# Local attention in a 13-stage decoder: queries and keys made with tokens on partitions, normalised and rotated there, then turned

## The chip, the cores and the metric

One core of a Trainium2 chip runs the whole program. The metric is the device time of one execution in microseconds (us). TensorE multiplies matrices and writes into the eight PSUM banks (128 partitions by 512 f32 each), VectorE (DVE in the profile) and ScalarE (ACT) read PSUM and SBUF, GpSimd (POOL) works on SBUF, SyncE (SP) issues the DMAs. Every engine runs its own queue in order; semaphores order the queues against each other.

## What is computed

The reference is a chain of thirteen stages (four groups of attention, cross attention and feed-forward, all on 4 x 256 tokens of width 128). The change touches the last group's local transformer, which has two layers, `L3_ffn0` and `L3_ffn1`. Cut to what matters:

```python
h = shift_token(x)                       # [1024 tokens, 128]
q, k, v = split(h @ wqkv, 3)             # 8 heads x 64 each
q = l2norm(q) * q_scale                  # over the 64 of a head
k = l2norm(k) * k_scale
q = q * cos * scale + rotate_half(q) * sin * scale
k = k * cos / scale + rotate_half(k) * sin / scale
o = local_attention(q * 8, k, v)         # windows of 64 keys back
x = x + o @ wo
```

`rotate_half` puts the negated upper 32 of a head's 64 in place of the lower 32, and the lower 32 in place of the upper.

## The kernel before

Each stage is a function; the stages run one behind the other, each as a few blocks, and all engines meet between blocks. `x` is kept in SBUF with its 128 features on partitions and its 1024 tokens along the free axis. `L3_ffn` (line 2455) shifts the tokens (`shift_tokens`), makes q, k and v in the block at lines 2476 to 2591, runs `attention` on them (line 379, not touched; the call is at line 2592), adds the result to `x` and runs the feed-forward part. The block at 2476 to 2591 is what changes.

It makes q and k already turned: features of one pair of heads on 128 partitions, 512 tokens along the free axis. There are 16 items, each a side (q or k), one of 4 head pairs `g` and one half `h` of the tokens; they go in 8 pairs of items. For an item TensorE makes two products of 128x512, one with the weights `wqk` and one with `wqk_swapped`, whose columns are those of the other half of each head (line 2504). That swap is the crossed term of the rotation. ScalarE squares the straight product (2538), TensorE sums the squares of each head over partitions with the constant `head_sum` (2516), VectorE bounds the sum from below (2578), ScalarE takes Ln and Exp(-0.5 .) (2527, 2530). VectorE multiplies both products with tables of cosines and sines (2569), GpSimd adds the two (2590), and VectorE multiplies with the inverse norm and 8 or 1 into `q` or `k` (2557). Once in each pair TensorE also makes one tile of v, 128 tokens by 512 (2509), and VectorE copies it (2575).

The order of each queue is written out by hand. TensorE's for a pair: four products (an item waits until VectorE has rotated the item two before it, `turned`), the v product, then the two head sums (each waits for `squared`). VectorE's for a pair: four rotations, the v copy, two bounds, then `finish` of the pair before. The item's products use banks 0 to 3, head sums 4 and 5, v 6 and 7, so that two items, two sums and two v tiles are in flight.

Weights come in one pack for each stage, loaded into one of two arenas while the stage before works (`fetch_next`, line 71); the constants (`constants`, line 2637, with the four cosine and sine tables and `head_sum`) are one more load, the sixth DMA of the start, which GpSimd alone waits for (line 1029).

Of the kernel before, what the change touches and what calls it, by code (L numbers as in the profile page):

```python
# [21 lines left out]
ALU = mybir.AluOpType  # L22
AX = mybir.AxisListType

P = 128
# [958 lines left out]
def halves(ap):  # L984
    return [ap[:, h * HALF:(h + 1) * HALF] for h in range(2)]
# [1469 lines left out]
def L3_ffn(K, layer):  # L2455
# [8 lines left out]
    with ExitStack() as stack:  # L2464
# [8 lines left out]
        with ExitStack() as attn:  # L2473
            q, k = sb("q", [P, NG, T], attn), sb("k", [P, NG, T], attn)
            v = sb("v", [P, 2 * B, H * DH], attn)
            with ExitStack() as inner:
                sem = Sems(nc, inner, tag + "_qk")
                product_done, squared, norm_done, rooted = (sem(n) for n in ("product_done", "squared", "norm_done",
                                                                             "rooted"))
                own, turned, summed, finished = sem("dve_own"), sem("turned"), sem("summed"), sem("finished")  # L2480
                bounded, logged = sem("bounded"), sem("logged")
                v_done, v_taken = sem("v_done"), sem("v_taken")
                square, norm = sb("square", [P, 2, HALF], inner), sb("norm", [P, 4, HALF], inner)
                part = sb("part", [P, 4, 2, HALF], inner)
                table = sb("table", [P, 4, S], inner)
                block = inner.enter_context(nc.Block())

                items = [(side, g, h) for side in range(2) for g in range(NG) for h in range(2)]  # L2490
                pairs = [(j, j + 1) for j in range(0, len(items), 2)]
                assert len(pairs) == 2 * B

                @block.tensor
                def _(pe):
                    for p, pair in enumerate(pairs):
                        for j in pair:
                            side, g, h = items[j]
                            if j >= 2:

                                pe.wait_ge(turned, j - 1)
                            for n, name in enumerate(("wqk", "wqk_swapped")):
                                at = side * NG * P + g * P
                                last = nc.tensor.matmul(K.bank[2 * (j % 2) + n][:], W(name)[:, at:at + P],  # L2504
                                                        halves(shifted)[h], start=True, stop=True)
                            last.then_inc(product_done, 1)
                        if p >= 2:
                            pe.wait_ge(v_taken, p - 1)
                        nc.tensor.matmul(K.bank[6 + p % 2][:], shifted[:, p * P:(p + 1) * P], W("wv"),
                                         start=True, stop=True).then_inc(v_done, 1)  # L2510
                        for j in pair:
                            pe.wait_ge(squared, j + 1)
                            if j >= 2:

                                pe.wait_ge(bounded, j - 1)
                            nc.tensor.matmul(K.bank[4 + j % 2][:], K.w("head_sum"), square[:, j % 2],
                                             start=True, stop=True).then_inc(norm_done, 1)

                @block.scalar
                def _(act):  # L2520
                    nc.scalar.preload_act_table_set(LN_EXP)

                    def invert(pair):

                        for j in pair:
                            act.wait_ge(bounded, j + 1)
                            nc.scalar.activation(norm[:, j % 4], norm[:, j % 4], ACT.Ln).then_inc(logged, 1)
                        for j in pair:
                            act.wait_ge(logged, j + 1)
                            nc.scalar.activation(norm[:, j % 4], norm[:, j % 4], ACT.Exp, scale=-0.5).then_inc(rooted, 1)  # L2530

                    for p, pair in enumerate(pairs):
                        for j in pair:
                            act.wait_ge(product_done, j + 1)
                            if j >= 2:

                                act.wait_ge(norm_done, j - 1)
                            nc.scalar.activation(square[:, j % 2], K.bank[2 * (j % 2)][:], ACT.Square
                                                 ).then_inc(squared, 1)
                        if p >= 1:  # L2540
                            invert(pairs[p - 1])
                    invert(pairs[-1])

                @block.vector
                def _(dve):
                    chain = Chain(dve, own)
                    for n, (tab, sc) in enumerate((("cos_lq", "q_scale"), ("sin_lq", "q_scale_swapped"),
                                                   ("cos_lk", "k_scale"), ("sin_lk", "k_scale_swapped"))):
                        last = nc.vector.tensor_scalar(table[:, n], K.w(tab), W(sc), None, ALU.mult)
                    chain.link(last)  # L2550

                    def finish(j):
                        side, g, h = items[j]
                        dve.wait_ge(rooted, j + 1)
                        dve.wait_ge(summed, j + 1)
                        dst = (q, k)[side][:, g, h * HALF:(h + 1) * HALF]
                        nc.vector.scalar_tensor_tensor(out=dst, in0=part[:, j % 4, 0], scalar=(8.0, 1.0)[side],
                                                       in1=norm[:, j % 4], op0=ALU.mult, op1=ALU.mult).then_inc(finished, 1)

                    for p, pair in enumerate(pairs):  # L2560
                        for j in pair:
                            side = items[j][0]

                            dve.wait_ge(squared, j + 1)
                            if j >= 4:

                                dve.wait_ge(finished, j - 3)
                            for n in range(2):
                                last = nc.vector.tensor_tensor(  # L2569
                                    part[:, j % 4, n].rearrange("p (b s) -> p b s", b=2),  # L2570
                                    K.bank[2 * (j % 2) + n][:].rearrange("p (b s) -> p b s", b=2),
                                    table[:, 2 * side + n].unsqueeze(1).to_broadcast([P, 2, S]), ALU.mult)
                            last.then_inc(turned, 1)
                        dve.wait_ge(v_done, p + 1)
                        nc.vector.tensor_copy(v[:, p], K.bank[6 + p % 2][:]).then_inc(v_taken, 1)
                        for j in pair:
                            dve.wait_ge(norm_done, j + 1)
                            nc.vector.tensor_scalar(norm[:, j % 4], K.bank[4 + j % 2][:], 1e-24, None, ALU.max
                                                    ).then_inc(bounded, 1)
                        if p >= 1:  # L2580
                            for j in pairs[p - 1]:
                                finish(j)
                    for j in pairs[-1]:
                        finish(j)

                @block.gpsimd
                def _(pool):
                    for j in range(len(items)):
                        pool.wait_ge(turned, j + 1)
                        nc.gpsimd.tensor_tensor(part[:, j % 4, 0], part[:, j % 4, 0], part[:, j % 4, 1], ALU.add  # L2590
                                                ).then_inc(summed, 1)
# [45 lines left out]
def constants():  # L2637
# [10 lines left out]
         "head_sum": np.kron(np.eye(2, dtype=f), np.ones((64, 64), f)), "guard": np.full((P, 1), -math.log(GUARD), f)}  # L2648
    c["band"] = np.concatenate([np.where((col <= row + sc * P) & (col >= row + sc * P - 64), 0, MASKED).astype(f)
                                for sc in range(2)], 1)  # L2650

    half_idx = np.arange(0, 64, 2, dtype=f)
# [5 lines left out]
    sign = np.repeat(np.array([-1, 1], f), 32)  # L2658
    for side, sc in (("q", scale), ("k", f(1.0) / scale)):
        for n, fn, sg in (("cos", np.cos, 1), ("sin", np.sin, sign)):  # L2660
            one = np.concatenate([fn(freqs).astype(f) * sc] * 2, 1) * sg
            c[f"{n}_l{side}"] = np.tile(one.astype(f), (1, 2)).T
    return c
# [32 lines left out]
def parameters(i):  # L2696
# [93 lines left out]
    for l in range(2):  # L2790
        g, wqkv = f"L3_ffn{l}.", i["L3_ffn_wqkv"][l]
        other = np.arange(1024) ^ 32
        p[g + "wqk"], p[g + "wqk_swapped"], p[g + "wv"] = wqkv[:, :1024], wqkv[:, other], wqkv[:, 1024:]
        p[g + "wo"] = chunks(i["L3_ffn_wo"][l])
        for n in "qk":
            sc = i[f"L3_ffn_{n}_scale"][l]
# [54 lines left out]
```

## Time and profile before

| | |
|---|---|
| median of 3 runs | 1531.03 us (1525.84 to 1531.7) |
| the profiled execution | 1537.08 us |
| its span, first to last instruction | 1535.1 us |
| mean granted TensorE clock | 0.921 of full |
| changed block, layer 0 | 1235.1 to 1288.8 us |
| changed block, layer 1 | 1383.3 to 1435.4 us |

A row of the timeline is: start in us, duration in us, engine, line of the kernel, operation, output and inputs, count, and in brackets how long the engine was idle before it and who released it. PE is a matmul, PEld a weight load. An f32 matmul of 512 columns appears as two records, here called passes, each with its weight load. The modelled durations of PE records overlap, so passes are read from start to start.

### The profile page before, as it was taken

To read this page: it belongs to the slowest core of one execution; us is meant where nothing else is said; L and a number is where in the kernel's file an instruction comes from. 1 tells how busy PE (TensorE), PEld (TensorE's weight loads), DVE (VectorE), ACT (ScalarE), POOL (GpSimd) and SP (SyncE) were. 2 spreads that over 40 slices of the span, in tenths; PEclk is the share of its full clock that TensorE was granted. 3 is DMA by queue.
4 is the path that set the end of the run, shared out by engine and by line. 5 is a ranking of instruction groups with operands and counts; after the bars stand their busy time and mean duration, and the time that the engine had idled before them with its cause. 6 is when DMAs were issued, how large, how long until landed. Compare 5 with 4: busy or idle time off the path is not lost. (4 is left out here: it accounts for less than half of the span.)

```text
span 1535.1 us, 21303 instructions
## 1 busy us (share of the span) xinstructions
PE 1242.6 (81%) x7118; PEld 627.0 (41%) x7118; DVE 965.0 (63%) x1980; ACT 883.3 (58%) x1827; POOL 541.0 (35%) x673
## 2 busy tenths in 40 slices
PE   8999678166666677997878998967979988979886
PEld 3576443022222223553334653433454434624552
DVE  3674444999999955742667745546547567628752
ACT  3674234599999944875223874144736746524643
POOL 1463023488888855210004114011212134404440
PEclk9999977589999998998899999988999999989999
DMA  4000000000000005300105300014115010000000
GB/s 154 2 2 1 30 9 0 1 0 0 0 0 1 0 1 177 65 1 34 42 0 190 65 2 18 0 40 117 21 65 150 9 57 1 1 1 1 1 1 14
DMA packets 44109, 49.02 MB, mean 32 GB/s; under 512 B 3809, under 2 KB 40801, under 8 KB 42721
## 3 DMA queue, kind: packets, MB, share of 16 engines
q1 hardware_dynamic: 40688, 46.10, 10.4%
q10 hardware_dynamic: 3312, 1.57, 0.4%
q8 instruction: 57, 0.93, 0.3%
q14 instruction: 52, 0.42, 0.1%
HBM read 34.55 MB, written 13.11 MB: 31 GB/s over the span
## 5 line engine op out<-in xcount | busy, mean ns | idle before, releaser
L1597 POOL TENSOR_TENSOR L_attn_z<-L_attn_state,L_attn_r 128x1024 f32<-128x1024 f32 x64 | 151.0, 2361 | 21.8 <-DVE L_attn_state L1583 15.0
L1583 DVE TENSOR_TENSOR_SCAN L_attn_state<-bank,L_attn_w 128x512 f32<-128x512 f32 x128 | 148.9, 1204 | 0.0
L1494 PE MATMUL bank<-L_attn_z,const 128*128 128x512 f32 x256 | 138.8, 670 | 1.4 <-POOL L_attn_z L1601 1.4
L953 DVE CUSTOM_DVE_ANT_0 L_xattn_core_logits<-bank,L_xattn_mask 128x256 f32<-128x256 f32 x256 | 98.4, 422 | 42.0 <-PE bank L722 30.1
L1478 PE MATMUL bank<-L_attn_rows,L_attn_select 128*128 128x512 bf16 x96 | 36.8, 441 | 79.1 <-ACT L_attn_C L1546 42.5
L1534 ACT ACTIVATE L_attn_r<-L_attn_after_dt,L_attn_half_guard,L_attn_A 128x512 f32<-128x512 f32 x128 | 96.6, 803 | 0.0
L1524 ACT ACTIVATE bank<-L_attn_dt,L_attn_A 128x510 f32<-128x510 f32 x128 | 86.6, 677 | 12.7 <-DVE L_attn_state L1583 12.7
L865 ACT ACTIVATE L_xattn_core_probs<-bank 128x512 f32<-128x512 f32 x132 | 71.6, 596 | 30.3 <-PE bank L765 21.4
L1601 POOL TENSOR_TENSOR L_attn_z<-L_attn_z,L_attn_C 128x1024 f32<-128x1024 f32 x32 | 75.8, 2368 | 23.1 <-ACT L_attn_C L1546 23.0
L1564 DVE TENSOR_TENSOR L_attn_w<-bank,L_attn_udt 128x1024 f32<-128x1024 f32 x64 | 78.2, 1221 | 5.0 <-PE bank L1478 1.6
L1494 PEld LDWEIGHTS bank<-L_attn_z,const 128*128 128x128 f32 x256 | 54.0, 212 | 50.3 <-issue 39.5
L543 POOL TENSOR_TENSOR L_attn_core_probs<-L_attn_core_probs,L_attn_core_rsum 128x256 f32<-128x256 f32 x64 | 51.7, 829 | 60.8 <-DVE L_attn_core_rsum L512 60.8
L543 POOL TENSOR_TENSOR L_ffn_core_probs<-L_ffn_core_probs,L_ffn_core_rsum 128x256 f32<-128x256 f32 x64 | 51.6, 828 | 45.5 <-DVE L_ffn_core_rsum L512 45.5
L1540 ACT ACTIVATE L_attn_r<-L_attn_r 128x1024 f32<-128x1024 f32 x64 | 66.8, 1043 | 0.0
L2504 PE MATMUL bank<-L_ffn_shifted,weights 128*128 128x512 f32 x128 | 59.4, 607 | 8.2 <-PEq L2423 8.2
L722 PE MATMUL bank<-L_xattn_core_rows 48*128 48x256 bf16 x384 | 55.3, 277 | 8.8 <-DVE L_xattn_core_top L953 4.1
L2590 POOL TENSOR_TENSOR L_ffn_part<-L_ffn_part 128x512 f32<-128x512 f32 x32 | 40.8, 1275 | 59.6 <-DVE L_ffn_part L2569 59.6
L923 POOL TENSOR_TENSOR shiftsT<-L_xattn_core_top,nothing 128x8 bf16<-128x8 f32 x48 | 12.1, 252 | 134.7 <-DVE L_xattn_core_top L953 92.3
L1478 PEld LDWEIGHTS bank<-L_attn_rows,L_attn_select 128*128 128x128 bf16 x96 | 7.8, 104 | 121.7 <-ACT L_attn_C L1546 56.0
L477 ACT ACTIVATE L_ffn_core_probs<-bank,L_ffn_core_negmax 128x128 f32<-128x128 f32 (+1 forms) x128 | 52.1, 427 | 9.2 <-DVE L_ffn_core_negmax L503 9.2
L957 DVE TENSOR_REDUCE L_attn_core_top<-bank 128x2 f32<-128x512 f32 x64 | 40.7, 684 | 24.1 <-PE bank L722 23.6
L477 ACT ACTIVATE L_attn_core_probs<-bank,L_attn_core_negmax 128x128 f32<-128x128 f32 (+1 forms) x128 | 52.0, 425 | 3.9 <-DVE L_attn_core_negmax L503 3.9
(518 smaller groups left out, 3098.2 us busy)
## 6 DMA issues: line engine op xcount, KB each, us to landing
L_xattn_core_rows<-L_xattn_core_slots SPq DMA_DIRECT2D x48, 96.0 KB, 2.3
L_xattn_core_rows<-L_xattn_core_slots SPq DMA_DIRECT2D x12, 384.0 KB, 5.5
weights<-in_pack_L_ffn SPq DMA_DIRECT2D x2, 2118.5 KB, 8.5
L_xattn_core_slots<-L_xattn_core_k_parts SPq DMA_DIRECT2D x24, 128.0 KB, 2.1
weights<-in_pack_L_ffn SPq DMA_DIRECT2D x1, 2824.0 KB, 12.0
L_xattn_core_slots<-L_xattn_core_q_parts SPq DMA_DIRECT2D x9, 192.0 KB, 2.2
weights<-in_pack_L_xattn SPq DMA_DIRECT2D x1, 1539.5 KB, 6.6
weights<-in_pack_L_attn SPq DMA_DIRECT2D x2, 768.0 KB, 9.9
```

What stands on the lines that cost most here:

```text
L477: last = nc.scalar.activation(probs[:, i % NB, side, columns[sc]], scores_bank[2 * (i % 2) + side][:, columns[sc]], ACT.Exp, bias=negmax[: ...
L543: last = nc.gpsimd.tensor_tensor(part, part, rsum[:, i % NB, :, sc:sc + 1].to_broadcast([P, 2, keys[sc].stop]), ALU.mult)
L865: nc.scalar.activation(probs[n % 3][:, at], shifted_bank[at][:], ACT.Exp).then_inc(exp_done, 1)
L953: last = nc.vector.tensor_tensor_reduce(logits[:, c], scores_bank[side][:, c * S:(c + 1) * S], mask[:, 2 * b + c, :], 1.0, MASKED, ALU.add ...
L1494: last = nc.tensor.matmul(y_bank[2 * c + half][:], ident, z[:, g % NS, c], start=False, stop=False, skip_group_check=True)
L1524: nc.scalar.activation(two(a_bank[c][:])[:, :, lo:lo + S - 1], two(dt[d][:, c, tokens(half)])[:, :, lo:lo + S - 1], ACT.Exp, scale=A[d][:, ...
L1534: last = nc.scalar.activation(r[:, g % NS, c], after_dt[d][:, c, tokens(half)], ACT.Tanh, bias=half_guard[:], scale=A[d][:, 1, at:at + 1])
L1540: nc.scalar.activation(r[:, g % NS], r[:, g % NS], ACT.Copy, scale=0.5, bias=0.5).then_inc(r_done, 1)
L1564: nc.vector.tensor_tensor(w[:, g % 2], B_bank[:].unsqueeze(1).to_broadcast([P, DC, HALF]), udt[d][:, :, tokens(half)], ALU.mult).then_inc( ...
L1583: nc.vector.tensor_tensor_scan(state[:, g % NS, c, ::step], a_bank[c][:, ::step], w[:, g % 2, c, ::step], 0.0, ALU.mult, ALU.add).then_inc ...
L1597: nc.gpsimd.tensor_tensor(z[:, g % NS], state[:, g % NS], r[:, g % NS], ALU.mult).then_inc(z_done, 1)
L1601: nc.gpsimd.tensor_tensor(z[:, g % NS], z[:, g % NS], copied[:, g // 2 % 2].unsqueeze(1).to_broadcast([P, DC, HALF]), ALU.mult).then_inc(p ...
```

## The change

The block makes q and k with tokens on partitions. There are 8 tiles of 128 tokens. For a tile TensorE makes three products of 128x512 with the tokens as the stationary operand: all of q, all of k, all of v. ScalarE squares q and k and copies v; VectorE rotates (the crossed term is read from the same product, with a table whose halves are swapped), sums the squares of each of the 16 heads along the free axis (one reduction of 1024 elements to 16), bounds the 16 sums, and multiplies the rotated 1024 elements with the 16 inverse norms. GpSimd adds straight and crossed halves in two instructions. TensorE then turns the tile with eight 128x128 products against the identity, and ScalarE copies the two turned banks into `q` and `k`. `wqk_swapped`, `head_sum` and the four tables leave the packs; `angles` (512 columns) and `scale_rows` (128 columns) join each layer's pack. The factor 8 moves into the table. Products of two tiles use banks 0 to 5, the turned tiles banks 6 and 7.

The new queues, from the diff (removed lines are those of lines 2477 to 2591 above and are left out):

```diff
+                    def products(t):
+                        if t >= 2:
+                            pe.wait_ge(rotated, t - 1)
+                            pe.wait_ge(v_taken, t - 1)
+                        weights = (W("wqk")[:, 0:HALF], W("wqk")[:, HALF:2 * HALF], W("wv"))
+                        for n in range(3):
+                            last = nc.tensor.matmul(bank_of(t, n)[:], shifted[:, t * P:(t + 1) * P], weights[n],
+                                                    start=True, stop=True)
                             last.then_inc(product_done, 1)
...
+                    products(0)
+                    for t in range(TILES):
+                        if t + 1 < TILES:
+                            products(t + 1)
+                        pe.wait_ge(normed, t + 1)
+                        for side in range(2):
+                            if t >= 1:
+                                pe.wait_ge(turns_taken, 2 * (t - 1) + side + 1)
+                            for g in range(NG):
+                                at = side * HALF + g * P
+                                last = nc.tensor.matmul(turn_bank[side][:, g * P:(g + 1) * P], rows[:, t % 2, at:at + P],
+                                                        K.w("ident"), start=True, stop=True)
+                            last.then_inc(turned, 1)
...
+                    squares(0)
+                    for t in range(TILES):
+                        act.wait_ge(product_done, 3 * t + 3)
+                        nc.scalar.activation(v[:, t], bank_of(t, 2)[:], ACT.Copy).then_inc(v_taken, 1)
+                        if t + 1 < TILES:
+                            squares(t + 1)
+                        roots(t)
+                        if t >= 1:
+                            take_turned(t - 1)
+                    take_turned(TILES - 1)
...
+                    def norms(t):
+                        dve.wait_ge(rooted, t + 1)
+                        dve.wait_ge(added, t + 1)
+                        if t >= 2:
+                            dve.wait_ge(turned, 2 * (t - 1))
+                        nc.vector.tensor_tensor(heads(rows[:, t % 2]), heads(part[:, t % 2, 0]),
+                                                norm[:, t % 2].unsqueeze(2).to_broadcast([P, HEADS, DH]), ALU.mult
+                                                ).then_inc(normed, 1)
+
+                    for t in range(TILES):
+                        for side in range(2):
+                            dve.wait_ge(squared, 2 * t + side + 1)
+                            if t >= 2:
+                                dve.wait_ge(normed, t - 1)
                             for n in range(2):
                                 last = nc.vector.tensor_tensor(
+                                    heads(part[:, t % 2, n, side * HALF:(side + 1) * HALF]), heads(bank_of(t, side)[:]),
+                                    table[:, side, n, t % 2].unsqueeze(1).to_broadcast([P, H, DH]), ALU.mult)
+                        last.then_inc(rotated, 1)
+                        chain.link(nc.vector.tensor_reduce(norm[:, t % 2], heads(square[:, t % 2]), AX.X, ALU.add))
+                        nc.vector.tensor_scalar(norm[:, t % 2], norm[:, t % 2], 1e-24, None, ALU.max).then_inc(bounded, 1)
+                        if t >= 1:
+                            norms(t - 1)
+                    norms(TILES - 1)
...
+                    for t in range(TILES):
+                        pool.wait_ge(rotated, t + 1)
+                        straight, crossed = heads(part[:, t % 2, 0]), heads(part[:, t % 2, 1])
+                        for lo, hi in ((0, DEEP), (DEEP, DH)):
+                            other = slice(DEEP, DH) if lo == 0 else slice(0, DEEP)
+                            last = nc.gpsimd.tensor_tensor(straight[:, :, lo:hi], straight[:, :, lo:hi],
+                                                           crossed[:, :, other], ALU.add)
+                        last.then_inc(added, 1)
```

`squares(t)` squares the q and the k product of tile t, each behind its own product; `roots(t)` is Ln and Exp on 16 columns; `take_turned(t)` copies the two turned banks, 128x512 each. Ahead of the loop VectorE makes the table with four instructions of 128x128.

## Rows read from the trace of the kernel before

**Rows 1.** The page, part 1: busy time of each engine over the whole span.

```profile
PE 1242.6 (81%) x7118; PEld 627.0 (41%) x7118; DVE 965.0 (63%) x1980; ACT 883.3 (58%) x1827; POOL 541.0 (35%) x673
```

**Rows 2.** Busy time by windows: the changed stage in layer 0, then in layer 1.

```profile
core 0: us, PE busy (x) PEld busy (x) DVE busy (x) ACT busy (x) POOL busy (x), PEclk, DMA share, GB/s
1235.10:1288.80 53.70, 49.97 (x112) 21.84 (x112) 45.77 (x76) 27.62 (x49) 20.38 (x16) 0.97 0.08 33
1383.30:1435.40 52.10, 48.30 (x112) 21.16 (x112) 45.77 (x76) 27.59 (x49) 20.41 (x16) 1.00 0.00 1
```

**Rows 3.** Timeline of the changed stage, layer 0, one period: start us, us, engine, line.

```profile
1272.50 0.19 PEld L2504 LDWEIGHTS bank<-L_ffn_shifted,weights 128*128 128x128 f32 x1 [0.24 <-DVE L_ffn_part L2569]
...
1274.84 0.60 ACT L2538 ACTIVATE L_ffn_square<-bank 128x512 f32<-128x512 f32 x1 [1.62 <-PE bank L2504]
...
1275.47 1.29 DVE L2569 TENSOR_TENSOR L_ffn_part<-bank,L_ffn_table 128x512 f32<-128x512 f32 x2
...
1278.51 0.19 PEld L2504 LDWEIGHTS bank<-L_ffn_shifted,weights 128*128 128x128 f32 x1 [0.24 <-DVE L_ffn_part L2569]
```

**Rows 4.** Timeline of L3_xattn: 16 passes that turn eight 128x128 blocks.

```profile
1135.85 1.87 PEld L2310 LDWEIGHTS bank<-const,L_xattn_pick 128*128 128x128 f32 x16
```

**Rows 5.** Timeline of L0_ffn: row sums, bound, broadcast product, then 16 turning passes.

```profile
189.91 1.22 DVE L1178 TENSOR_REDUCE L_ffn_scale<-L_ffn_rows 128x8 f32<-128x1024 f32 x1
191.16 0.17 DVE L1179 TENSOR_SCALAR L_ffn_scale<-L_ffn_scale 128x8 f32<-128x8 f32 x1
...
191.61 1.23 DVE L1183 TENSOR_TENSOR L_ffn_ints<-L_ffn_rows,L_ffn_inverse 128x1024 f32<-128x1024 f32 x1
...
195.16 3.53 PEld L163 LDWEIGHTS bank<-const,L_ffn_ints 128*128 128x128 f32 x16
```

**Rows 6.** TensorE by windows: us, busy (x), granted clock, DMA share, GB/s.

```profile
1235.10:1238.50 3.40, 3.36 (x4) 0.50 0.93 394
...
1355.20:1359.20 4.00, 0.02 (x1) 0.84 0.00 0
1359.20:1365.00 5.80, 5.80 (x7) 0.52 0.00 0
...
194.80:199.30 4.50, 4.18 (x18) 0.50 0.00 0
...
1380.30:1383.20 2.90, 0.00 (x0) 1.00 0.00 0
1383.30:1387.00 3.70, 3.70 (x9) 1.00 0.00 0
```

**Rows 7.** Groups by line, changed stage, layer 0: xcount | busy us, mean ns | idle.

```profile
L2569 DVE TENSOR_TENSOR L_ffn_part<-bank,L_ffn_table 128x512 f32<-128x512 f32 x32 | 20.6, 686 | 7.9 <-ACT L_ffn_square L2538 7.8
L2590 POOL TENSOR_TENSOR L_ffn_part<-L_ffn_part 128x512 f32<-128x512 f32 x16 | 20.4, 1274 | 30.6 <-DVE L_ffn_part L2569 30.6
```

**Rows 8.** Timeline of its start in layer 0: TensorE begins, ScalarE takes the first item.

```profile
1235.14 5.33 PE L2504 MATMUL bank<-L_ffn_shifted,weights 128*128 128x512 f32 x8 [5.19 <-PEq L2423]
...
1238.79 0.60 ACT L2538 ACTIVATE L_ffn_square<-bank 128x512 f32<-128x512 f32 x1 [2.41 <-PE bank L2504]
```

**Rows 9.** Timeline of L1_attn: VectorE and GpSimd side by side, all from SBUF.

```profile
264.66 1.03 POOL L1356 CAST L_attn_middle<-L_attn_left 32x1024 bf16<-32x1024 f32 x1
264.67 1.06 DVE L1392 TENSOR_SCALAR L_attn_A<-L_attn_A 128x32 f32<-128x32 f32 x1
...
266.86 0.18 DVE L1392 TENSOR_SCALAR L_attn_A<-L_attn_A 128x32 f32<-128x32 f32 x1
266.87 2.16 POOL L1358 TENSOR_TENSOR L_attn_rows<-L_attn_left,L_attn_middle 32x1024 bf16<-32x1024 f32 x1
...
267.08 3.03 DVE L1397 SCALAR_TENSOR_TENSOR L_attn_dt<-L_attn_dt,L_attn_spare 128x1024 f32<-128x1024 f32 x1
...
274.36 1.19 DVE L1397 SCALAR_TENSOR_TENSOR L_attn_dt<-L_attn_dt,L_attn_spare 128x1024 f32<-128x1024 f32 x1
```

**Rows 10.** DMA issues of the first 60 us: count, KB each, us to landing.

```profile
const<-in_pack_const SPq DMA_DIRECT2D x1, 1346.0 KB, 11.1
```

More of the change, by code:

```diff
@@ L2476, in L3_ffn @@
             with ExitStack() as inner:
[L2477 to L2482, printed above, removed]
@@ L2483, in L3_ffn @@
-                square, norm = sb("square", [P, 2, HALF], inner), sb("norm", [P, 4, HALF], inner)
-                part = sb("part", [P, 4, 2, HALF], inner)
-                table = sb("table", [P, 4, S], inner)
+                sem = Sems(nc, inner, tag + "_qkv")
+                own, table_ready, product_done, squared, rotated = (sem(n) for n in (
+                    "dve_own", "table_ready", "product_done", "squared", "rotated"))
+                added, bounded, act_own, rooted = (sem(n) for n in ("added", "bounded", "act_own", "rooted"))
@@ new lines, in L3_ffn @@
+                normed, turned, v_taken, turns_taken = (sem(n) for n in ("normed", "turned", "v_taken", "turns_taken"))
+                TILES, HEADS, DEEP = 2 * B, 2 * H, DH // 2
+                table = sb("table", [P, 2, 2, 2, DH], inner)
+                square = sb("square", [P, 2, 2 * HALF], inner)
+                part = sb("part", [P, 2, 2, 2 * HALF], inner)
+                rows = sb("rows", [P, 2, 2 * HALF], inner)
+                norm = sb("norm", [P, 2, HEADS], inner)
+                heads = lambda ap: ap.rearrange("p (h d) -> p h d", d=DH)
@@ L2486, in L3_ffn @@
+                bank_of = lambda t, n: K.bank[3 * (t % 2) + n]
+                turn_bank = K.bank[6:8]
                 block = inner.enter_context(nc.Block())
-                items = [(side, g, h) for side in range(2) for g in range(NG) for h in range(2)]
-                pairs = [(j, j + 1) for j in range(0, len(items), 2)]
-                assert len(pairs) == 2 * B
                 @block.tensor
                 def _(pe):
[L2496 to L2505, printed above, removed]
-                            last.then_inc(product_done, 1)
[L2507 to L2517, printed above, removed]
@@ L2521, in _ @@
                     nc.scalar.preload_act_table_set(LN_EXP)
[L2523 to L2541, printed above, removed]
@@ L2542, in _, with squares @@
-                    invert(pairs[-1])
+                    def squares(t):
+                        for side in range(2):
+                            act.wait_ge(product_done, 3 * t + side + 1)
+                            if t >= 2:
+                                act.wait_ge(bounded, t - 1)
+                            nc.scalar.activation(square[:, t % 2, side * HALF:(side + 1) * HALF], bank_of(t, side)[:],
+                                                 ACT.Square).then_inc(squared, 1)
@@ new lines, in roots, with take_turned @@
+                    def roots(t):
+                        act.wait_ge(bounded, t + 1)
+                        nc.scalar.activation(norm[:, t % 2], norm[:, t % 2], ACT.Ln).then_inc(act_own, 1)
+                        act.wait_ge(act_own, t + 1)
+                        nc.scalar.activation(norm[:, t % 2], norm[:, t % 2], ACT.Exp, scale=-0.5).then_inc(rooted, 1)
+                    def take_turned(t):
+                        for side in range(2):
+                            act.wait_ge(turned, 2 * t + side + 1)
+                            nc.scalar.activation((q, k)[side][:, :, t * P:(t + 1) * P],
+                                                 turn_bank[side][:].rearrange("p (g s) -> p g s", g=NG), ACT.Copy
+                                                 ).then_inc(turns_taken, 1)
@@ L2546, in _ @@
                     chain = Chain(dve, own)
[L2547 to L2567, printed above, removed]
+                    base = W("angles").rearrange("p (s n c d) -> p s n c d", s=2, n=2, c=2)
+                    scales = W("scale_rows").rearrange("p (s d) -> p s d", s=2)
+                    for side in range(2):
+                        for n in range(2):
+                            nc.vector.scalar_tensor_tensor(
+                                out=table[:, side, n], in0=base[:, side, n], scalar=(8.0, 1.0)[side],
+                                in1=scales[:, side].unsqueeze(1).to_broadcast([P, 2, DH]), op0=ALU.mult, op1=ALU.mult
+                                ).then_inc(table_ready, 1)
@@ L2572, in _ @@
[L2572 to L2579, printed above, removed]
@@ L2661, in constants @@
             one = np.concatenate([fn(freqs).astype(f) * sc] * 2, 1) * sg
-            c[f"{n}_l{side}"] = np.tile(one.astype(f), (1, 2)).T
-    return c
+            one = one.astype(f)[:, np.arange(64) ^ (0 if n == "cos" else 32)]
+            tables.append(chunks(one))
+    return np.concatenate(tables, 1)
 def retention_constants():
@@ L2791, in parameters @@
         g, wqkv = f"L3_ffn{l}.", i["L3_ffn_wqkv"][l]
-        other = np.arange(1024) ^ 32
-        p[g + "wqk"], p[g + "wqk_swapped"], p[g + "wv"] = wqkv[:, :1024], wqkv[:, other], wqkv[:, 1024:]
+        p[g + "wqk"], p[g + "wv"] = wqkv[:, :1024], wqkv[:, 1024:]
+        p[g + "angles"] = local_angles()
+        p[g + "scale_rows"] = np.concatenate([rows(i[f"L3_ffn_{n}_scale"][l]) for n in "qk"], 1)
         p[g + "wo"] = chunks(i["L3_ffn_wo"][l])
-        for n in "qk":
-            sc = i[f"L3_ffn_{n}_scale"][l]
-            p[g + n + "_scale"], p[g + n + "_scale_swapped"] = column(np.tile(sc, 2)), column(np.tile(sc[np.arange(64) ^ 32], 2))
         p[g + "ln_g"], p[g + "ln_b"], p[g + "b2"] = (column(i["L3_ffn_" + n][l]) for n in ("ln_g", "ln_b", "b2"))
```

20 lines of the change are left out of this document (8 added, 12 removed).

## The prediction

> **What bounds the kernel now.** I read the page first: TensorE is busy 81% of the span [rows 1], but that mixes thirteen stages. The windows of the two layers show the changed block: 53.7 and 52.1 us, with TensorE busy in all but some 4 us of each and VectorE in 45.8 [rows 2]. The timeline gives the period: an item pair's first weight load starts at 1272.50 and the next pair's at 1278.51, 6.01 us [rows 3]. In it TensorE makes 14 passes (four products, one v product, two head sums, two passes each), 0.43 us a pass, with no hole. So TensorE bounds the block; VectorE, at 5.7 us a pair (45.8 / 8), is close behind and works beside it, because two item pairs overlap. The whole block is 105.8 us of 1535.
>
> **What is taken away and added, tile for pair (8 of each per layer).** TensorE loses 14 passes of 512 columns and gets 6 of them (2.58 us at full clock) and 16 turning passes of 128 columns. Eight blocks turned in the same form took 1.87 us at full clock [rows 4] and 3.53 us at the half clock [rows 5, 6]. VectorE keeps four rotations, which also read PSUM and a table (0.686 us each, 1.29 for two in a row [rows 3, 7]), drops the v copy and two full bounds and two finishes, and gets a sum over 1024 elements (1.22), a bound on 16 columns (0.17, taken from 8) and a broadcast product over 1024 elements (1.23) [rows 5]. That is 2.58 + 2.62 = 5.2 us of work. GpSimd keeps 1024 added elements, twice 1.27 us [rows 7]; its inner runs of 32 are my extrapolation. ScalarE's five copies and squares at 0.60 [rows 3] and two 16-column functions come to about 3.4 us and stay off the path. By work alone the block would shrink: 4.45 us on TensorE, 5.2 on VectorE, against 6.01.
>
> **What the order makes of it.** I follow the queues as written. TensorE issues the products of tile t+1, waits for `normed` of tile t, turns tile t, and only then issues the products of t+2. VectorE normalises tile t only behind the rotation of t+1, for which it needs those products. So each tile closes a ring through three engines, and TensorE idles while VectorE works, VectorE while TensorE turns. The ring, from the first pass of a tile's products:
>
> 1. First product visible to ScalarE: at half clock four passes and the hand-over took 3.65 us (1235.14 to 1238.79 [rows 8]), so a pass is 0.85 and the hand-over 0.24; two passes 1.95. At full clock 2 x 0.43 + 0.2 = 1.06.
> 2. Square, then VectorE: 0.63 (1274.84 to 1275.47 [rows 3]).
> 3. Four rotations: 2.58. The second square comes in time, at half clock up to 0.4 late.
> 4. Sum, bound, product: 1.22 + 0.03 + 0.17 + 0.05 + 1.23 = 2.70 if nothing disturbs them. But `rotated` starts GpSimd's two adds at the same moment. In the rows of L1_attn a product of two SBUF operands takes 1.19 alone, and 3.03 when it starts at 267.08 under a GpSimd instruction that ends at 269.03: it ends 1.08 after that one. A 32-column scalar operation from SBUF takes 0.18 alone and 1.06 beside GpSimd's 1.03 [rows 9]. So the bound waits for the first add (0.05 + 1.27 = 1.32) and ends at 1.50; the second add holds the product until 2.77, and it ends at 4.0. I take 4.0; ends of the range 2.7, and 5.25 if the sum over `square` too stands in GpSimd's way.
> 5. Hand-over 0.05 and the turning, 1.87 or 3.50.
>
> The clock decides between the two values. After its products TensorE has nothing for 5 us or more. In the trace of before a 4.0 us hole (1355.2 to 1359.2) is followed by 5.8 us at 0.52, that is 1.2 GHz nearly throughout, and one of 5.2 us (the idle time in the row at 1235.14) by 3.4 us at 0.50 [rows 6, 8]; a hole of 2.9 us (1380.3) is followed by 1.00, 2.4 GHz [rows 6]. So the turning runs at half clock, and as 3.4 to 5.8 us pass before the clock returns and the turning takes 3.5, the first product behind it mostly does too. The ring: 1.95 + 0.63 + 2.58 + 4.0 + 0.05 + 3.5 = **12.7 us a tile** instead of 6.01. At full clock it is 1.06 + 0.63 + 2.58 + 4.0 + 0.05 + 1.87 = 10.2.
>
> The Trainium skill (TensorE: Matmul & The Clock Gate, LDWEIGHTS) gives a load of 128 columns about 107 ns without regard to the clock; 16 would be 1.71 us at either level. The row at half clock has 3.53, so here row and page differ, and the row stands.
>
> The same skill (SBUF — State Buffer, two separate sides) has VectorE and GpSimd exclude each other where VectorE has two SBUF inputs or runs in a two-port mode. No row here shows whether a sum from SBUF is held; by that page it is not.
>
> **Sum, layer 0.** Start to the products of tile 2: first product 1.95, square 0.63, two rotations to 3.87; second product visible 3.65, its rotations 4.28 to 5.57; sum and bound to 7.1; tile 1's rotations to 9.7; step 4 to 13.7; turning to 17.2. Five rings of 12.7: 80.8, where tile 7's products start. Tile 6 is normed 9.2 later (90.0) and turned by 93.5; tile 7, normed meanwhile, is turned in some 2.9 (between 1.87 and 3.5): 96.4; hand-over and last copy 0.24 + 0.60: 97.2. Before 53.7: **+43.5**. Layer 1 starts at full clock, 1.3 less: 95.9 against 52.1, **+43.8**.
>
> Edits costed at nothing: the four table instructions (before four of VectorE at the start, after four of half the size) lie under the first product; the small functions of ScalarE end before step 4 does, and if late they would add their 0.4. The constants shrink by 1152 columns, 576 of 1346 KB [rows 10]; only GpSimd waits for them at the start, beside the first stage's products, and no queue moves. Were that cover gone, they could give at most 576 / 1346 of their 11.1 us to landing, 4.7 us. Each layer's pack is 388 columns smaller, loaded a stage ahead. The blocks behind start as before.
>
> Together +87: 1537.08 + 87.3 = 1624.4 for an execution like the profiled one, which lies 6.05 above the median of 1531.03; on the median's scale 1618.
>
> **Rivals.**
> - *The clock holds.* For: a hole of 2.9 us did no harm [rows 6]. Against: the hole is over 5 us. 2.5 us less for some 14 rings, -35: 1583. If the first product alone runs at full clock, 0.9 x 14 less: 1606, inside my forecast.
> - *Turning costs the same at half clock*, the page's rule: 3.5 - 1.87 less on 16 turnings, -26: 1592. The row speaks against it.
> - *GpSimd does not hold VectorE.* For: rotations read PSUM and a table beside GpSimd today and stay at 0.686 [rows 7]. Against: those have one SBUF operand. 4.0 becomes 2.7: -1.3 x 14 = -18: 1600. With the clock up as well: 1565.
> - *More is held, or GpSimd's short runs cost more:* +1.25 x 16 = +20: 1638.
> - *The ring is no ring (faster).* If the turning of t and the rotation of t+2 overlapped, VectorE's 5.3 us would be the period: 8 x 5.3 + 6 of filling = 48 against 53.7, about -10 in all, 1521; held by GpSimd, 6.5 x 8 + 6 = 58: +10, 1541, or about equal if the filling is shorter. It turns on TensorE's queue alone: as soon as products of t+2 stood ahead of the turning of t it would be so. They stand behind it.
>
> **How the numbers follow.** Forecast (ring, half clock, held) 0.57, between 1604 and 1630; clock holds 0.09; turning cheap 0.03; not held 0.14, both 0.04; more held 0.08; overlap without loss 0.03, about equal 0.02. Leaving out what lies above 1640 and below 1580 (both, the overlap) leaves under 2 in 10 outside. 0.5%, some 8 us, is about what a measurement of this kernel can tell from no change; faster takes the overlap, 0.03, same 0.02, slower the rest.
>
> **What would show it.** In the profile after: the changed block 90 to 100 us long in each layer; TensorE's weight loads of the turning released by VectorE's product, idle some 5 us before each, clock near 0.5 to 0.7; VectorE's four rotations 0.69 each; its 16-column bound over 1 us and the broadcast product near 2.5 instead of 1.23. If the block takes near 80 us, clock or hold was wrong; near 50, the ring was.

## The result, and the profile after

The changed kernel takes 1584.98 us (median of 4 runs, 1584.46 to 1585.5) against 1530.81 before (1525.84 to 1531.7): 1.0344 times as long, 95% interval 1.0314 to 1.0375. That is +54.2 us. The forecast was 1618, +87, in a range of 1580 to 1640: the direction and the place were right, and the rise forecast was 1.6 times the measured one.

The page's first part shows nothing of it. TensorE is busy as long as before [rows 1], in a span 48 us longer:

```profile
PE 1238.5 (78%) x7238; PEld 648.4 (41%) x7246; DVE 952.0 (60%) x1948; ACT 879.7 (56%) x1843; POOL 553.2 (35%) x673
```

The windows of the two blocks show all of it (us, busy time of each engine, granted clock, DMA share, GB/s; the second ends where the last copy ends). They answer to [rows 2]:

```profile
core 0: us, PE busy (x) PEld busy (x) DVE busy (x) ACT busy (x) POOL busy (x), PEclk, DMA share, GB/s
1231.60:1312.30 80.70, 51.33 (x176) 33.11 (x176) 40.55 (x60) 25.82 (x57) 27.26 (x16) 0.81 0.05 21
1404.10:1483.20 79.10, 49.12 (x176) 33.36 (x176) 40.44 (x60) 25.83 (x57) 27.21 (x16) 0.83 0.00 1
```

80.7 and 79.1 us against 53.7 and 52.1: +27.0 in each, +54.0 together. VectorE and ScalarE have less work than before (40.6 against 45.8, 25.8 against 27.6), and every engine is idle more than a third of the time: the mark of a wait that runs around, not of an engine that is full. The mean clock fell from 0.97 and 1.00 to 0.81 and 0.83. The profiled executions differ by only 47.8 us (1584.87 against 1537.08). Outside the blocks the changed one is 6.3 us shorter (1582.8 - 159.8 = 1423.0 against 1535.1 - 105.8 = 1429.3): 2.2 us of that lie in the attention behind the block (below), the rest in code that is the same in both. So it is partly luck that the 54.0 of the blocks and the 54.2 of the medians agree so closely.

One period of the changed block, layer 0, answers to [rows 3]. It is read as a ring: TensorE's loads of the turning, ScalarE's first square of the next tile, VectorE's four rotations, its sum, bound and broadcast product, and the next turning. GpSimd's two adds lie beside it.

```profile
1254.82 2.62 PEld L2515 LDWEIGHTS bank<-const,L_ffn_rows 128*128 128x128 f32 x16 [4.81 <-DVE L_ffn_rows L2573]
...
1259.43 0.60 ACT L2528 ACTIVATE L_ffn_square<-bank 128x512 f32<-128x512 f32 x1 [7.01 <-PE bank L2501]
...
1260.06 2.48 DVE L2583 TENSOR_TENSOR L_ffn_part<-bank,L_ffn_table 128x512 f32<-128x512 f32 x4 [5.29 <-ACT L_ffn_square L2528]
...
1262.46 1.21 DVE L2587 TENSOR_REDUCE L_ffn_norm<-L_ffn_square 128x16 f32<-128x1024 f32 x1
1262.62 3.54 POOL L2600 TENSOR_TENSOR L_ffn_part<-L_ffn_part 128x512 f32<-128x512 f32 x2 [6.73 <-DVE L_ffn_part L2583]
1263.71 0.20 DVE L2588 TENSOR_SCALAR L_ffn_norm<-L_ffn_norm 128x16 f32<-128x16 f32 x1
1263.82 1.22 DVE L2573 TENSOR_TENSOR L_ffn_rows<-L_ffn_part,L_ffn_norm 128x1024 f32<-128x1024 f32 x1
1265.10 2.65 PEld L2515 LDWEIGHTS bank<-const,L_ffn_rows 128*128 128x128 f32 x16 [4.81 <-DVE L_ffn_rows L2573]
```

The turnings start at 1254.82 and 1265.10: 10.28 us a tile instead of 6.01 a pair. The last row's bracket shows the wait: TensorE's loads had been idle 4.81 us and were released by VectorE's product of line 2573. The pieces: 4.61 from the turning to the first square, 0.63 to the rotations, 2.40 for them, 1.25 to the bound, 0.11 and 1.28 for the product and the hand-over.

TensorE's clock in that period (us, busy, clock), and the groups by line that answer to [rows 7]:

```profile
1260.70:1265.00 4.30, 0.41 (x1) 1.00 0.00 0
1254.80:1255.80 1.00, 0.98 (x8) 1.00 0.00 0
1255.80:1259.20 3.40, 3.40 (x12) 0.50 0.01 2
1259.20:1262.00 2.80, 1.91 (x5) 1.00 0.00 0
```

```profile
L2600 POOL TENSOR_TENSOR L_ffn_part<-L_ffn_part 128x512 f32<-128x512 f32 x16 | 27.3, 1726 | 48.7 <-DVE L_ffn_part L2583 48.7
...
L2583 DVE TENSOR_TENSOR L_ffn_part<-bank,L_ffn_table 128x512 f32<-128x512 f32 x32 | 20.0, 683 | 34.9 <-ACT L_ffn_square L2528 34.9
...
L2573 DVE TENSOR_TENSOR L_ffn_rows<-L_ffn_part,L_ffn_norm 128x1024 f32<-128x1024 f32 x8 | 9.7, 1216 | 1.2 <-POOL L_ffn_part L2600 1.2
L2587 DVE TENSOR_REDUCE L_ffn_norm<-L_ffn_square 128x16 f32<-128x1024 f32 x8 | 9.7, 1208 | 0.0
```

The stretch from 1260.70 to 1265.00, in which TensorE is idle but for its first 0.41 us, is granted 1.00, and so is the first microsecond of the turning; then come 3.4 us at 0.50, and 1.00 again. GpSimd's adds take 1726 ns on average instead of 1274: the first of the tile shown 1250 ns, the second 2335. VectorE's product takes 1216, what it takes alone [rows 5].

### The profile page after: what moved, and what is told of

Same layout as the page of the kernel before. It is cut to its first block and busy times, and to the rows that moved or that the text cites. A ratio compares the mean times of both kernels' runs of the same rounds, so it can differ in the third digit from the quotient of the medians.

```text
span 1582.8 us, 21515 instructions
## 1 busy us (share of the span) xinstructions
PE 1238.5 (78%) x7238; PEld 648.4 (41%) x7246; DVE 952.0 (60%) x1948; ACT 879.7 (56%) x1843; POOL 553.2 (35%) x673
## 5 line engine op out<-in xcount | busy, mean ns | idle before, releaser
L2515 PE MATMUL bank<-const,L_ffn_rows 128*128 128x128 f32 x256 | 49.4, 375 | 57.9 <-DVE L_ffn_rows L2573 57.9
L2600 POOL TENSOR_TENSOR L_ffn_part<-L_ffn_part 128x512 f32<-128x512 f32 x32 | 54.5, 1724 | 95.8 <-DVE L_ffn_part L2583 95.8
L1564 DVE TENSOR_TENSOR L_attn_w<-bank,L_attn_udt 128x1024 f32<-128x1024 f32 x64 | 78.2, 1221 | 5.0 <-remote 0.9
L2583 DVE TENSOR_TENSOR L_ffn_part<-bank,L_ffn_table 128x512 f32<-128x512 f32 x64 | 39.8, 682 | 68.2 <-ACT L_ffn_square L2528 68.2
L2515 PEld LDWEIGHTS bank<-const,L_ffn_rows 128*128 128x128 f32 x256 | 45.5, 277 | 69.5 <-DVE L_ffn_rows L2573 69.5
L2528 ACT ACTIVATE L_ffn_square<-bank 128x512 f32<-128x512 f32 x32 | 19.1, 597 | 94.9 <-PE bank L2501 94.7
L2501 PE MATMUL bank<-weights,L_ffn_shifted 128*128 128x512 f32 x96 | 53.5, 705 | 8.2 <-PEq L2423 8.2
```

The lines of the kernel that those rows point to most:

```text
L1564: nc.vector.tensor_tensor(w[:, g % 2], B_bank[:].unsqueeze(1).to_broadcast([P, DC, HALF]), udt[d][:, :, tokens(half)], ALU.mult).then_inc( ...
L2515: last = nc.tensor.matmul(turn_bank[side][:, g * P:(g + 1) * P], rows[:, t % 2, at:at + P], K.w("ident"), start=True, stop=True)
```

## The experiments

The first two ask whether the ring holds the loss and what the clock costs in it; the third and fourth what GpSimd has to do with it; the fifth cuts the ring on its other side; the last asks whether the smaller constants matter. Before ran 11 times beside the first job (median 1531.08) and 13 times beside the second (1531.96). Block lengths are given from the table load of ScalarE to the first instruction of `attention` on VectorE; in these terms before has 54.0 and 52.3, the changed kernel 81.0 and 79.3.

**The ring cut on TensorE.** The order of two lines:

```diff
                     products(0)
+                    products(1)
                     for t in range(TILES):
-                        if t + 1 < TILES:
-                            products(t + 1)
+                        if t + 2 < TILES:
+                            products(t + 2)
                         pe.wait_ge(normed, t + 1)
```

> The changed kernel with one change of order on TensorE: the products of tile t+2 are issued ahead of the turning of tile t. Ring theory: VectorE no longer waits for the turning, and its own 5.04 us a tile (2.40 of rotations, 2.64 of sum, bound and product) become the period instead of 10.27; each block goes from 80 us to about 48, the whole from 1585 to about 1521. TensorE's holes shrink below 1 us and its clock stays near 1.00. Rival, that GpSimd (3.5 us a tile, waiting and held) or ScalarE's queue takes the wait over: a period of 6.5 or more, 1541 or above. Rival, that the loss is not the ring but the slower single steps: nothing gained, 1585.

Measured: 1515.83 us (1506.42 to 1521.55, 6 runs), 0.9908 of before, interval 0.9879 to 0.9936. Blocks of 47.8 and 47.9 us. The timeline of two tiles:

```profile
1245.45 1.21 DVE L2588 TENSOR_REDUCE L_ffn_norm<-L_ffn_square 128x16 f32<-128x1024 f32 x1
...
1246.82 1.21 DVE L2574 TENSOR_TENSOR L_ffn_rows<-L_ffn_part,L_ffn_norm 128x1024 f32<-128x1024 f32 x1
...
1248.09 1.86 PEld L2516 LDWEIGHTS bank<-const,L_ffn_rows 128*128 128x128 f32 x16 [1.29 <-DVE L_ffn_rows L2574]
...
1248.14 2.48 DVE L2584 TENSOR_TENSOR L_ffn_part<-bank,L_ffn_table 128x512 f32<-128x512 f32 x4
...
1250.54 1.21 DVE L2588 TENSOR_REDUCE L_ffn_norm<-L_ffn_square 128x16 f32<-128x1024 f32 x1
...
1251.92 1.21 DVE L2574 TENSOR_TENSOR L_ffn_rows<-L_ffn_part,L_ffn_norm 128x1024 f32<-128x1024 f32 x1
```

The turning and the next rotations now start together (1248.09, 1248.14), and sums follow each other by 5.09 us (1245.45, 1250.54). The windows, one of ten microseconds inside the block and the two blocks whole:

```profile
1236.00:1246.00 10.00, 9.07 (x45) 5.68 (x44) 9.72 (x15) 5.99 (x14) 6.94 (x5) 1.00 0.00 1
...
1221.00:1268.80 47.80, 38.95 (x176) 23.68 (x176) 40.62 (x61) 26.71 (x57) 27.38 (x16) 0.96 0.08 35
1359.50:1407.30 47.80, 39.83 (x176) 25.96 (x176) 40.50 (x60) 26.64 (x57) 27.36 (x16) 0.93 0.00 1
```

VectorE is busy 9.72 of 10 us and the clock is 1.00 in the ten microseconds. So the place of one call in TensorE's queue holds 33 of the block's 81 us, and with it moved the kernel is 0.9% faster than that of before: its work is smaller, as the sum by work alone had it (5.2 us a tile on VectorE against 6.01 a pair on TensorE). GpSimd, the rival, has time left (busy 6.94 of the 10 us).

**TensorE kept busy in its hole.** The ring stays; three products that nothing reads fill the wait:

```diff
                             products(t + 1)
+                        if t >= 1:
+                            pe.wait_ge(turns_taken, 2 * t)
+                        for n in range(3):
+                            nc.tensor.matmul(turn_bank[n % 2][:], shifted[:, 0:P], W("wv"), start=True, stop=True)
                         pe.wait_ge(normed, t + 1)
```

> The changed kernel with three more products of 128x512 in each tile, into the turned tile's banks, whose result nothing reads, issued while TensorE waits for the normalised tile: its hole shrinks from 4.4 us to about 1.5. Clock theory: the turning and the first product then run at full clock, and from the first turning load to the first square it takes 2.9 us instead of 4.61; 14 rings of 1.7 give 23 us, 1562. Rival, that the 4.61 us are not the clock's: 1585 or a little above, with more work on TensorE.

Measured: 1567.12 us (1565.08 to 1568.79, 4 runs), ratio 1.0237 (1.0203 to 1.027), 18 us less than the changed kernel, with 24 products more in each layer. The added products (line 2512), the turning, the first square, and the next turning:

```profile
1258.27 2.84 PE L2512 MATMUL bank<-weights,L_ffn_shifted 128*128 128x512 f32 x6 [1.16 <-ACT L_ffn_k L2544]
...
1261.10 1.86 PEld L2519 LDWEIGHTS bank<-const,L_ffn_rows 128*128 128x128 f32 x16 [0.82 <-DVE L_ffn_rows L2577]
...
1264.05 0.60 ACT L2532 ACTIVATE L_ffn_square<-bank 128x512 f32<-128x512 f32 x1 [5.34 <-PE bank L2501]
...
1269.72 1.86 PEld L2519 LDWEIGHTS bank<-const,L_ffn_rows 128*128 128x128 f32 x16 [0.82 <-DVE L_ffn_rows L2577]
```

From turning to first square it is 2.95 us, the price forecast for full clock (1.87 + 1.06 = 2.93), and the period is 8.62. The clock thus costs 1.66 us a ring, 23 in 14 rings. The whole gained 18, because the last tile's turning of each layer now stands behind three products that do not help it:

```profile
1297.66 0.60 ACT L2544 ACTIVATE L_ffn_k<-bank 128x512 f32<-128x512 f32 x1 [0.30 <-PE bank L2519]
...
1298.31 2.84 PE L2512 MATMUL bank<-weights,L_ffn_shifted 128*128 128x512 f32 x6 [0.69 <-ACT L_ffn_k L2544]
...
1300.56 0.19 PEld L2519 LDWEIGHTS bank<-const,L_ffn_rows 128*128 128x128 f32 x1 [0.24 <-issue]
```

VectorE's product for this tile ended at 1297.96, so without them the turning would have begun about 2.5 us before 1300.56; twice that is the 5 us between 23 and 18.

**GpSimd's adds as one instruction:**

```diff
-                        for lo, hi in ((0, DEEP), (DEEP, DH)):
-                            other = slice(DEEP, DH) if lo == 0 else slice(0, DEEP)
-                            last = nc.gpsimd.tensor_tensor(straight[:, :, lo:hi], straight[:, :, lo:hi],
-                                                           crossed[:, :, other], ALU.add)
-                        last.then_inc(added, 1)
+                        nc.gpsimd.tensor_tensor(straight, straight, crossed, ALU.add).then_inc(added, 1)
```

> The changed kernel with GpSimd's two adds of 512 elements made one of 1024, which starts at the same moment and leaves the swap of the halves out (another sum, same count of elements). Holding theory: VectorE's bound and broadcast product must wait until the whole add is over, at 2.6 us behind the rotation instead of 1.25: 1.3 more in each of 14 rings, 18 us, 1603. Rival, that GpSimd never holds VectorE and only VectorE holds GpSimd: 1585, with a longer GpSimd instruction.

Measured: 1602.12 us (1600.08 to 1603.82, 4 runs), 17 more than the changed kernel, ratio 1.0466 (1.0431 to 1.05). ScalarE's first square, VectorE's sum, GpSimd's add, VectorE's bound and product, and the turning:

```profile
1260.13 0.60 ACT L2528 ACTIVATE L_ffn_square<-bank 128x512 f32<-128x512 f32 x1 [9.01 <-PE bank L2501]
...
1263.16 1.21 DVE L2587 TENSOR_REDUCE L_ffn_norm<-L_ffn_square 128x16 f32<-128x1024 f32 x1
1263.32 2.34 POOL L2598 TENSOR_TENSOR L_ffn_part<-L_ffn_part 128x1024 f32<-128x1024 f32 x1 [9.93 <-DVE L_ffn_part L2583]
1264.40 1.29 DVE L2588 TENSOR_SCALAR L_ffn_norm<-L_ffn_norm 128x16 f32<-128x16 f32 x1
1265.61 1.21 DVE L2573 TENSOR_TENSOR L_ffn_rows<-L_ffn_part,L_ffn_norm 128x1024 f32<-128x1024 f32 x1
...
1266.88 3.37 PEld L2515 LDWEIGHTS bank<-const,L_ffn_rows 128*128 128x128 f32 x16 [5.78 <-DVE L_ffn_rows L2573]
```

The bound of 16 columns takes 1.29 us instead of 0.20 and ends at 1265.69, with GpSimd's add (1263.32 + 2.34 = 1265.66). The product starts only then. So GpSimd does hold VectorE, as forecast; what decides is where its instruction ends. From the sum to the turning it is 3.72 us (1263.16 to 1266.88) instead of 2.64: 1.08 more, not the 1.3 expected. The ring grew by more, from 10.4 to 11.8 us on the mean of six in layer 0, because the longer hole also brought more half clock. In every other ring the clock had fallen before the hole ended (0.50 from 1253.5 on), and from the turning, which began at 1254.60, to the first square it was 5.53 us; in the ring behind it, 4.57. The blocks are 91.4 and 90.1 us, 21 more together, while the totals differ by 17: that 1603 was expected and 1602 came is in part chance.

**The second add left out:**

```diff
-                        for lo, hi in ((0, DEEP), (DEEP, DH)):
+                        for lo, hi in ((0, DEEP),):
```

> The changed kernel with the second of GpSimd's two adds left out (the upper halves of each head miss their crossed term). If the second add costs VectorE nothing inside the ring, only the last tile's product, which waited 1.2 us for it, comes earlier: 1.2 in each layer, about 1582.5. If it costs VectorE something in each tile: 5 us less or more.

Measured: 1578.2 us (1573.69 to 1580.07, 4 runs), ratio 1.0303 (1.0268 to 1.0338). By the total alone this would speak for the second case, 7 us less. The block says otherwise: 80.4 and 79.0 us, 0.6 and 0.3 less than the changed kernel, and inside a ring the steps are the same:

```profile
1260.15 1.21 DVE L2587 TENSOR_REDUCE L_ffn_norm<-L_ffn_square 128x16 f32<-128x1024 f32 x1
1260.31 1.25 POOL L2600 TENSOR_TENSOR L_ffn_part<-L_ffn_part 128x512 f32<-128x512 f32 x1 [8.97 <-DVE L_ffn_part L2583]
1261.39 0.20 DVE L2588 TENSOR_SCALAR L_ffn_norm<-L_ffn_norm 128x16 f32<-128x16 f32 x1
1261.50 1.22 DVE L2573 TENSOR_TENSOR L_ffn_rows<-L_ffn_part,L_ffn_norm 128x1024 f32<-128x1024 f32 x1
```

Sum to bound 1.24, bound 0.20, product 0.11 behind it: as with two adds. The last tile's product did come 1.2 us earlier, but its turning waits behind that of the tile before. The other 6 us lie outside the block, in code that is the same. Such differences show in every pair of profiles here: the block's start lies anywhere between 1221 and 1235 us, and a profiled execution up to 9 us off its kernel's median. So where totals differ by a few us, the lengths of the blocks decide.

**The ring cut on VectorE instead.**

```diff
-                        if t >= 1:
-                            norms(t - 1)
-                    norms(TILES - 1)
+                        norms(t)
...
+                        roots(t)
                         if t + 1 < TILES:
                             squares(t + 1)
-                        roots(t)
```

> The changed kernel with the ring cut on the other side: VectorE normalises tile t right behind its bound, ahead of the rotation of tile t+1, and ScalarE takes the roots of t ahead of the squares of t+1. TensorE's order stays. Ring theory: turning and rotation then overlap, and the period is rotation 2.40, GpSimd's two adds 2.6, product 1.25, that is 6.3 us: each block about 56 us instead of 80, 1537. Rival, that the order on VectorE does not matter: 1585.

Measured: 1538.43 us (1529.26 to 1543.45, 10 runs), ratio 1.0024 (0.9998 to 1.0051); blocks of 57.2 and 56.3 us. Rotations, GpSimd's adds, the product, the next rotations:

```profile
1255.71 2.48 DVE L2583 TENSOR_TENSOR L_ffn_part<-bank,L_ffn_table 128x512 f32<-128x512 f32 x4
...
1258.27 2.49 POOL L2598 TENSOR_TENSOR L_ffn_part<-L_ffn_part 128x512 f32<-128x512 f32 x2 [3.79 <-DVE L_ffn_part L2583]
...
1260.85 1.23 DVE L2573 TENSOR_TENSOR L_ffn_rows<-L_ffn_part,L_ffn_norm 128x1024 f32<-128x1024 f32 x1 [1.28 <-POOL L_ffn_part L2598]
...
1261.99 2.48 DVE L2583 TENSOR_TENSOR L_ffn_part<-bank,L_ffn_table 128x512 f32<-128x512 f32 x4
```

The period is 6.28 us, the forecast 6.3 (rotations start at 1255.71 and 1261.99): now the adds stand in VectorE's way for 1.3 us a tile, and that is about all that parts this version from the one with the ring cut on TensorE (5.09 us a tile, blocks of 47.8).

**The constants at their old size.**

```diff
+    c["unused"] = np.zeros((P, P + 4 * S), f)
```

> The changed kernel with 1152 unused columns of zeros put back into the constants, so that their load is 1346 KB again. Theory: nobody on the path waits for that load, 1585 within 2. Rival, that the smaller load brought the start forward: 1 to 5 us more.

Measured: 1584.41 us (1581.69 to 1586.12, 4 runs), ratio 1.0344 (1.0308 to 1.038), that of the changed kernel, and blocks of 81.0 and 79.3 us as there. The load of the constants has its 1346.0 KB again. The smaller load is worth nothing that these runs can tell.

## Why the prediction was right in kind and too large in size

*The ring* was right: TensorE's loads wait for VectorE's product. The cut on TensorE removes the whole loss, the one on VectorE 24 of the 27 us of layer 0 (81.0 to 57.2, against 54.0). The rival that there is no ring got its answer from the same runs: it is what the kernel does once two lines change places, at 5.09 us a tile (I had 5.3) and 1516 us (I had 1521).

*Step 4, the hold, failed in its size.* It said that the bound waits for the first add, and that the second add then holds the product: 4.0 us and 0.05. Measured 2.64 (1262.46 to 1265.10), which is the lower end, 2.70. The hold is real, as the single add shows. But the bound arrives at 1263.71 and the first add ends some 0.1 us later; VectorE then has its bound and, right behind it, its product in line, and it is GpSimd's second add that waits, to 2.34 us at the longest instead of 1.25. Such a second add by itself, from the run with the ring cut on TensorE:

```profile
1241.74 2.34 POOL L2601 TENSOR_TENSOR L_ffn_part<-L_ffn_part 128x512 f32<-128x512 f32 x1
```

VectorE's product ran there from 1241.73 to 1242.94; the add ended 1.14 us behind it. I had let the second add start between bound and product, without a row that says who of two waiting engines goes first. The sum was not held (1208 ns beside the first add), as the 4.0 had it. That the first add of 1.25 us ends just as the sum of 1.21 does is chance: with both adds made one, the step took 1.08 more. Too much by 1.4 a ring.

*Steps 1 and 5, the clock, failed in their size too.* Turning and first product together: 5.45 forecast at half clock, 2.93 at full, 4.61 measured. I had taken the hole to end at half clock, as in [rows 6]. It does not: the clock falls a microsecond into the turning and is back just before the first square, 3.4 us of each period. 0.84 a ring too much. The first turning of layer 0 lies at half clock:

```profile
1243.64 3.49 PEld L2515 LDWEIGHTS bank<-const,L_ffn_rows 128*128 128x128 f32 x16 [5.62 <-DVE L_ffn_rows L2573]
```

The loads take 3.49 there against 1.86 at 1.00 in the experiment with added products (1261.10). From this turning to the first square it is 5.52 us, against 5.45 forecast:

```profile
1249.16 0.60 ACT L2528 ACTIVATE L_ffn_square<-bank 128x512 f32<-128x512 f32 x1 [9.47 <-PE bank L2501]
```

The loads had been idle 5.62 us before it, and the clock stood at 0.50 from 1242.5 to 1243.6, within the hole. So the price of half clock was right; what failed is that every ring would pay all of it. The two errors hang together: I had reckoned with holes 1.4 us longer, by the hold that did not come. In the other rings the loads are idle 4.81 us, and the clock falls later. With the adds made one the holes are longer, and every other ring takes 5.53 us from turning to square. The hole's length alone does not decide it: there idle times of 5.90 and 5.78 us stood before 5.53 and 4.57 us. The Trainium skill (TensorE: Matmul & The Clock Gate, LDWEIGHTS) gives a load a time that does not depend on the clock; these rows show otherwise, and so do two loads that stand by themselves between products of the period above, 0.34 us at 0.50 (1258.38) and 0.19 at 1.00 (1259.66); the measurement decides.

*Step 3* was 2.40 for 2.58 (four in a row overlap more than twice two), *step 2* exact. Together 1.41 + 0.84 + 0.18 = 2.43: 12.7 becomes 10.27. The blocks were forecast 16.5 us (97.2 - 80.7) and 16.8 us (95.9 - 79.1) too long. In layer 0 that is 1.7 up to the first turning, 1.5 in the first ring, 2.4 in each of the next five, and 1.1 behind the last. The two make 33.3 of the 39.5 us by which the profiled execution was missed (1624.4 against 1584.87); 2.2 are in the term left out below, and 4 in code that is the same. On the medians the error is 33.

*Luck.* The measured 1585 lies inside the range, 5 us from its end, and outside the 1604 to 1630 that had the chance of 0.57. It falls on the 1583 of the rival "the clock holds", but the clock did not hold: the number came from two steps that were each too large, by 1.41 and 0.84 us a ring, with the clock still low in a third of it. Of the signs named, the idle loads (4.81 us) and the rotations (0.683) came; the bound over 1 us (0.20), the product near 2.5 (1.22), the clock of 0.5 to 0.7 (0.81 and 0.83) and the 90 to 100 us did not. "Near 80 us, clock or hold was wrong" came, and both were, in part.

*What was costed at nothing* held: constants, the table, ScalarE's functions, GpSimd's short runs of 32 (1.25 us for 512 elements, 1.27 in one run before).

*A term that the sum left out:* the block behind. Before, TensorE's loads were idle 5.3 us until VectorE's cast of the mask (line 498) released those of `attention` (line 421), and TensorE then worked at 0.55 and 0.68 for 4.5 us:

```profile
1289.58 0.87 PEld L421 LDWEIGHTS bank<-L_ffn_k,L_ffn_q 64*128 64x128 f32 x8 [5.31 <-DVE L_ffn_core_mask_bf L498]
```

```profile
1289.50:1291.50 2.00, 1.92 (x11) 0.55 0.05 12
1291.50:1294.00 2.50, 2.31 (x15) 0.68 0.00 0
```

With the change they are idle 1.6 us and start at 1.00:

```profile
1313.07 0.52 PEld L421 LDWEIGHTS bank<-L_ffn_k,L_ffn_q 64*128 64x128 f32 x8 [1.61 <-DVE L_ffn_core_mask_bf L498]
```

```profile
1312.80:1315.00 2.20, 1.93 (x20) 1.00 0.02 4
1315.00:1317.00 2.00, 0.99 (x12) 1.00 0.00 0
```

From the mask's cast to the next table load that makes 58.2 us instead of 59.3 in both layers, 1.1 us back each. With the ring cut on VectorE, where TensorE began `attention` at 0.50 (1285 to 1287), the same stretch took 59.5 us in layer 0, which speaks for the clock as the cause of the 1.1 us.

## What to carry to other kernels

Before you add up work, draw the order: if engine A issues step t+2 behind something that needs engine B's step t, and B does that step behind t+1, one tile's time is the sum over the engines and not the longest of them, and no engine is full. A second buffer does not help while the queue keeps the products behind the wait; look for the producer that can be issued one tile earlier, which here was the order of two lines and 64 of the two blocks' 160 us. Where GpSimd and VectorE both work from SBUF, cut GpSimd's work into instructions that end where VectorE arrives; here one long add instead of two short ones cost 17 us.

## What the runs showed of the hardware

In the profile of before the clock had fallen within the hole (0.84 in the one at 1355.2, [rows 6]), and so it had before the changed kernel's first turning (0.50 from 1242.5 to 1243.6). In the rings of 10.28 us behind it, it fell only about 1 us after TensorE had begun again (1.00 from 1260.7 to 1265.0 and from 1254.8 to 1255.8, then 0.50 to 1259.2), once in each; with three products in the hole and idle stretches of 1.16 and 0.82 us left, it stayed at 1.00 (window 1244.6 to 1302 of that experiment, in layer 0).

VectorE's sum over 1024 elements from SBUF and GpSimd's add ran side by side, at 1208 ns and 1.25 us; a sum over 1024 elements without GpSimd beside it took 1.22 [rows 5]. A 16-column bound from SBUF beside GpSimd took up to 1.29 us, and ended with GpSimd's instruction. VectorE's bound, waiting as GpSimd's first add ended, went before the second add, and so did the product right behind the bound, though the second add was in line by then; why VectorE kept its turn is not shown.
